# Row additions of one expert two in flight, pair lists fetched by ScalarE, last stage in place: a decoder layer with a sparse expert stage

## What is computed

```python
logits = flat @ router_w.T
scores = jax.nn.softmax(logits, axis=-1)
_, topk_idx = jax.lax.top_k(logits + router_bias, TOPK)
topk_scores = jnp.take_along_axis(scores, topk_idx, axis=-1)
topk_scores = topk_scores / topk_scores.sum(-1, keepdims=True)
combine = jnp.einsum('nk,nke->ne', topk_scores, jax.nn.one_hot(topk_idx, N_EXPERTS, dtype=scores.dtype))
out = jnp.zeros_like(flat)
for e in range(N_EXPERTS):
    h = jax.nn.silu(flat @ Wu[e]) * (flat @ Wg[e])
    out = out + combine[:, e:e + 1] * (h @ Wd[e])
out = out + jax.nn.silu(flat @ Su[0]) * (flat @ Sg[0]) @ Sd[0]
x = _layernorm(x + out.reshape(B, T, D), axis=-1)
```

## Time and profile before

| | |
|---|---|
| median of three runs (lowest, highest) | 2169.67 us (2161.83, 2170.12) |
| the profiled execution's own time, its span | 2160.96 us, 2159.3 us |
| stage 1, stage 2, stage 3 in the profile | to 1596, to 2106.8, to 2159.3 us |
| PE busy over the span | 1878.9 us (87%) |
| POOL busy; its idle time before L1407 | 767.0 us (36%); 152.8 us |
| ACT busy, DVE busy | 651.8 us (30%), 1194.9 us (55%) |
| additions, gathers, pair lists on POOL | 80 each; 1615, 983, 952 ns of POOL each |
| bytes moved in stage 3 | 16.79 MB |

### The profile page before, as it was taken

How to read it: one execution, slowest core, us unless ns; L and a number is a source line. 1 busy time by engine, 2 the same in 40 slices (tenths; PEclk the granted TensorE clock), 3 DMA queues, 4 the chain that set the end, 5 groups by cost and what they waited for, 6 DMA issues and landing times. The chain is left out here.

```text
span 2159.3 us, 35007 instructions
## 1 busy us (share of the span) xinstructions
PE 1878.9 (87%) x11010; PEld 1190.8 (55%) x11011; DVE 1194.9 (55%) x2460; ACT 651.8 (30%) x1357; POOL 767.0 (36%) x831
## 2 busy tenths in 40 slices
PE   3878999999999999999999999998759999999950
PEld 2456575766657566575766657576534544445420
DVE  2567776677667666766667676676422222222214
ACT  0152332424234242333424233241302212212214
POOL 3124233242323324233232323222235655655520
PEclk8889999999999999999999999998889999999985
DMA  7244243433423444142433424332035576565538
GB/s 235 55 111 105 53 103 78 105 99 66 115 61 94 103 91 115 40 115 71 94 99 84 115 59 96 83 82 60 21 156 110 125 197 170 90 149 114 94 52 311
DMA packets 142245, 225.35 MB, mean 104 GB/s; under 512 B 23360, under 2 KB 98112, under 8 KB 139456
## 3 DMA queue, kind: packets, MB, share of 16 engines
q1 hardware_dynamic: 101616, 132.94, 24.3%
q0 software_dynamic: 40528, 91.41, 18.2%
HBM read 94.70 MB, written 47.25 MB: 66 GB/s over the span
## 5 line engine op out<-in xcount | busy, mean ns | idle before, releaser
L1502 PE MATMUL ps<-ug_w,rowsT 128*128 x640 | 293.0, 601 | 6.8 <-SPq L1377 4.5
L1502 PEld LDWEIGHTS ps<-ug_w,rowsT 128*128 128x128 f32 x640 | 122.9, 193 | 163.0 <-issue 163.0
L950 DVE RECIPROCAL arden<-ps 128x256 f32<-128x256 f32 x64 | 112.5, 1758 | 143.8 <-PE ps L1274 140.3
L1017 PE MATMUL ps<-wqkv_sb,xT_sb 128*128 128x256 f32 (+1 forms) x512 | 173.7, 493 | 15.5 <-ACT maskr_sb L520 15.5
L1407 POOL DMA_INDIRECT sum_rows<-y_sb,pairs x80 | 129.2, 1615 | 152.8 <-DMA sum_rows<-y_sb,pairs 120.6
L470 POOL DMA_INDIRECT routed_ids<-pair_w,pos_w x64 | 64.0, 1000 | 328.2 <-DVE pair_w L741 291.0
L1458 DVE SCALAR_TENSOR_TENSOR silu<-tanh,ps 128x256 f32<-128x256 f32 x80 | 33.7, 421 | 256.3 <-ACT tanh L1425 256.3
L922 DVE SCALAR_TENSOR_TENSOR weighted<-ps,decay 128x384 f32<-128x384 f32 x256 | 140.4, 554 | 63.0 <-PE ps L1143 48.0
L905 DVE TENSOR_REDUCE smax<-ps 128x2 f32<-128x512 f32 x256 | 164.0, 682 | 17.0 <-PE ps L1200 17.0
L637 ACT ACTIVATE probs<-ps 128x1024 f32<-128x1024 f32 x128 | 130.9, 1025 | 116.2 <-PE ps L1251 116.1
L616 ACT ACTIVATE decay<-ps,g_col 128x256 f32<-128x256 f32 x256 | 121.6, 475 | 134.8 <-PE ps L1126 89.4
(11 more groups left out here) (239 smaller groups left out, 3913.4 us busy)
## 6 DMA issues: line engine op xcount, KB each, us to landing
q_stack<-qkT_hi SPq DMA_DIRECT2D x128, 128.0 KB, 3.8
mk_stack<-ctxT_hi SPq DMA_DIRECT2D x128, 128.0 KB, 4.9
mq_stack<-qkT_hi SPq DMA_DIRECT2D x128, 128.0 KB, 2.5
ug_w<-in_expert_ug SPq DMA_DIRECT2D x16, 1024.0 KB, 6.1
xT_sb<-in_xT SPq DMA_DIRECT2D x16, 512.0 KB, 3.4
x_sb<-in_x POOLq DMA_DIRECT2D x16, 512.0 KB, 4.0
ctxT_sb<-in_ctxT POOLq DMA_DIRECT2D x16, 512.0 KB, 3.7
q_stack<-qkT_lo SPq DMA_DIRECT2D x64, 128.0 KB, 4.4
```

Source lines behind the costliest of these rows:

```text
L950: nc.vector.reciprocal(arden[:, :], ps[:, 6 + c % 2, cols]).then_inc(arden_done.sem, 1)
L1017: ins = nc.tensor.matmul(ps[:, 2 * t + lo // 512, 0:hi - lo], xT_sb[:, c, P * t:P * t + P], wqkv_sb[:, c, lo:hi], start=c == 0, stop=c == ...
L1502: ins = nc.tensor.matmul(ps[:, 2 + k % 2, :], rowsT[:, k % 2, c, :], ug_w[:, bass.ds(slot, 1), c, :].rearrange("p o n -> p (o n)"), start= ...
```

## The change

**Additions.** Two semaphores `ey_added0` and `ey_added1` take turns, by the parity of the tile. Addition m waits until addition m - 2 has landed, and for m - 1 up to a number that stands in a new table `turns`: 16 times the additions of the other parity up to m - 3 where tile m belongs to the same expert as m - 1, and one more where the expert changes or where tile m is past the last used one. So with the 74 used tiles 59 additions need not wait for the one right before, and 21 must (or are the first): the 15 where an expert begins, and the six unused ones at the end, 74 to 79, which all go to the same spare rows. POOL reads the table's value from SBUF before each addition. LAG becomes 5.

**Pair lists.** Those of tiles 4 to 79 (and of four more that nobody uses) are fetched by ACT with a plain transfer at an address read from a new table `row0`; ACT issues it at the beginning of turns 0 to 3, and behind the copy of `rowsT` from turn 4 on. A gather waits for the new semaphores `later_in`.

**Tables.** DVE makes a third diagonal; PE's product (L1113) is 384 columns wide instead of 256; ten small operations for `row0` and `turns` are added behind the one that writes `idx`. `scored` and `ranks` move into the spare end of `hid`.

**Last stage.** `normalise` writes into `total` itself, and its wait for an earlier store is gone.

```diff
@@ -105,7 +105,8 @@
         def sem(name):
             return keep.enter_context(nc.semaphore(name))
 
-        tables = Tables(id_sb=sb("id_sb", [P, P]), idx=sb("idx", [P, MT], I32), pairs=sb("pairs", [P, MT, 2], I32),
+        tables = Tables(id_sb=sb("id_sb", [P, P]), idx=sb("idx", [P, MT], I32), pairs=sb("pairs", [P, MT + W, 2], I32),
+                        row0=sb("row0", [1, MT + W], I32), turns=sb("turns", [1, MT], I32),
                         weights=sb("weights", [1, MT], I32), slot=sb("slot", [1, MT], I32), ends=sb("ends", [1, E], I32),
                         pairs_in=[sem(f"pairs_in{q}") for q in range(W)], base_out=Signal(sem("base_out"), 16))
...
@@ -202,6 +203,8 @@
         hid_flat = hid[:, :, :, :].rearrange("p t h d -> p (t h d)")
         rope_a = hid_flat[:, 0:QKH * ROT].rearrange("p (h d) -> p h d", d=ROT)
         rope_b = hid_flat[:, QKH * ROT:2 * QKH * ROT].rearrange("p (h i two) -> p h i two", i=ROT // 2, two=2)
+        scored, ranks = (hid_flat[:, ST * H * HD - q * TOPK * ST * E:ST * H * HD - (q - 1) * TOPK * ST * E]
+                         .rearrange("p (k t e) -> p k t e", k=TOPK, e=E) for q in (1, 2))
         sq_flat = sq[:, :, :, :].rearrange("p t h d -> p (t h d)")
...
-                    for k in range(2):
+                    for k in range(3):
                         v.tensor_scalar(diag[:, k, :], id_sb[:, :], table[:, k:k + 1], None, ALU.mult).then_inc(diag_done.sem, 1)
 
...
                     dve.wait_ge(across_ready.sem, 1)
-                    v.tensor_copy(across, ps[:, 1, 0:2 * P].rearrange("p (k m) -> p k m", m=P)).then_inc(diag_done.sem, 1)
-                    dve.wait_ge(diag_done.sem, 3)
+                    v.tensor_copy(across, ps[:, 1, 0:3 * P].rearrange("p (k m) -> p k m", m=P)).then_inc(diag_done.sem, 1)
+                    dve.wait_ge(diag_done.sem, 4)
                     v.tensor_scalar(tables.idx[:, :], across[:, 0, 0:MT], row_p[:, :], None, ALU.add).then_inc(tables_done.sem, 1)
+                    v.tensor_copy(tables.row0[:, :], across[0:1, 0, 0:MT + W])
                     v.tensor_scalar(tables.weights[:, :], across[0:1, 1, 0:MT], 1.0, None, ALU.add)
+                    v.tensor_scalar(tables.ends[:, :], tiles_end[0:1, :], 1.0, None, ALU.add)
+
+                    v.tensor_tensor(change[:, 1:MT], across[0:1, 2, 1:MT], across[0:1, 2, 0:MT - 1], ALU.subtract)
+                    v.tensor_scalar(unused, across[0:1, 2, 0:MT], float(E - 1), None, ALU.subtract)
+                    v.tensor_scalar(half_i, iota_sb[0:1, 0:MT], 1.0, None, ALU.subtract)
                     v.tensor_copy(owner_i, across[0:1, 1, 0:MT]).then_inc(diag_done.sem, 1)
-                    v.tensor_scalar(tables.ends[:, :], tiles_end[0:1, :], 1.0, None, ALU.add)
-                    dve.wait_ge(diag_done.sem, 4)
+                    dve.wait_ge(diag_done.sem, 5)
                     v.tensor_scalar(tables.slot[:, :], owner_i, W - 1, None, ALU.bitwise_and)
+                    v.tensor_scalar(half_i, half_i, 1, None, ALU.arith_shift_right)
+                    v.tensor_tensor(change[:, 1:MT], change[:, 1:MT], unused[:, 1:MT], ALU.max).then_inc(diag_done.sem, 1)
+                    dve.wait_ge(diag_done.sem, 6)
+                    v.tensor_scalar(change[:, 1:MT], change[:, 1:MT], 0.0, 1.0, ALU.max, ALU.min).then_inc(diag_done.sem, 1)
+                    v.tensor_copy(unused, half_i).then_inc(diag_done.sem, 1)
+                    dve.wait_ge(diag_done.sem, 8)
+                    v.tensor_tensor(change[:, 1:MT], change[:, 1:MT], unused[:, 1:MT], ALU.add).then_inc(diag_done.sem, 1)
+                    dve.wait_ge(diag_done.sem, 9)
+                    v.tensor_scalar(tables.turns[:, 1:MT], change[:, 1:MT], 16.0, None, ALU.mult)
 
                 def hidden(c):
 
...
@@ -1109,8 +1126,8 @@
                     for c in range(1, SC):
                         ug(c)
                     if b is None and y is None:
-                        pe.wait_ge(diag_done.sem, 2)
-                        nc.tensor.matmul(ps[:, 1, 0:2 * P], ones_k[:, 0:1].to_broadcast([P, P]), sq_flat[:, 0:2 * P],
+                        pe.wait_ge(diag_done.sem, 3)
+                        nc.tensor.matmul(ps[:, 1, 0:3 * P], ones_k[:, 0:1].to_broadcast([P, P]), sq_flat[:, 0:3 * P],
                                          start=True, stop=True).then_inc(across_ready.sem, 1)
...
 
-    LAG = 7
+    LAG = 5
     with ExitStack() as ctx:
         def sb(name, shape, dt=F32):
...
+        later_in = [sem(f"later_in{s}") for s in range(W)]
 
         block = ctx.enter_context(nc.Block())
...
@@ -1392,29 +1410,37 @@
         def _(pool):
 
             def gather(m):
-                pool.wait_ge(tables.pairs_in[m % W], 16 * (m // W + 1))
-                if m >= W:
+                if m < W:
+                    pool.wait_ge(tables.pairs_in[m], 16)
+                else:
+                    pool.wait_ge(later_in[m % W], 16 * (m // W))
                     pool.wait_ge(rowsT_ready, m - W + 1)
                 pool.indirect_dma_start(out=rows[:, m % W, :], out_offset=None, in_=x2_dram,
                                         in_offset=bass.IndirectOffsetOnAxis(ap=tables.pairs[:, m, 0:1], axis=0)).then_inc(rows_in[m % W], 16)
 
             def add_up(m):
-                pool.wait_ge(y_done, m + 2)
-                if m >= 1:
-                    pool.wait_ge(y_added, 16 * m)
+
+                if m in (1, 2):
+                    pool.wait_ge(y_added[(m - 1) % 2], 16)
+                elif m > 2:
+                    turn = pool.value_load(tables.turns[0:1, m:m + 1], min_val=16, max_val=16 * MT)
+                    pool.wait_ge(y_added[m % 2], 16 * (m // 2))
+                    pool.wait_ge(y_added[(m - 1) % 2], turn)
                 else:
                     pool.wait_ge(tables.base_out.sem, 16 * B)
+                pool.wait_ge(y_done, m + 2)
                 pool.indirect_dma_start(out=sum_dram, out_offset=bass.IndirectOffsetOnAxis(ap=tables.pairs[:, m, 0:1], axis=0),
-                                        in_=y_sb[:, m % W, :], in_offset=None, compute_op=ALU.add).then_inc(y_added, 16)
+                                        in_=y_sb[:, m % W, :], in_offset=None, compute_op=ALU.add).then_inc(y_added[m % 2], 16)
 
             for m in range(MT + LAG):
                 if m < MT:
                     gather(m)
-                if m + W < MT:
-                    fetch_pairs(pool, ids_dram, tables, m + W)
                 if m >= LAG:
                     add_up(m - LAG)
-            pool.wait_ge(y_added, 16 * MT)
+            for s in range(2):
+                pool.wait_ge(y_added[s], 16 * (MT // 2))
+            for s in range(W):
+                pool.wait_ge(later_in[s], 16 * (MT // W))
 
         @block.scalar
         def _(act):
@@ -1437,13 +1463,24 @@
                     act.wait_ge(ug_ready, m - 1)
                 nc.scalar.copy(rowsT[:, k % 2, :, :], ps[:, k % 2, :].rearrange("p (c r) -> p c r", r=P)).then_inc(rowsT_done, 1)
 
+            def fetch(m, k):
+
+                of_m = slice(m, m + 1) if isinstance(m, int) else bass.ds(m, 1)
+                row = act.value_load(tables.row0[0:1, of_m], min_val=0, max_val=E * N)
+                pairs = tables.pairs[:, of_m, :].rearrange("p o two -> p (o two)")
+                act.dma_start(pairs, ids_dram[bass.ds(row, P), :]).then_inc(later_in[k % W], 16)
+
             def step(n, k):
+                if isinstance(n, int) and n < W:
+                    fetch(n + W, k + W)
                 if has(n, 1):
                     tanh(n - 1, k - 1)
                 if has(n, 2):
                     copy_hidT(n - 2, k - 2)
                 if has(n, 0):
                     copy_rowsT(n, k)
+                if not isinstance(n, int) or W <= n < MT:
+                    fetch(n + W, k + W)
 
             steps(act, step, 2)
...
-                    dve.wait_ge(y_added, 16 * (m - W + 1))
+                    rounds = (m - k) * 8 if not isinstance(m, int) else 0
+                    dve.wait_ge(y_added[k % 2], rounds + 16 * ((k - W) // 2 + 1))
                 of_row = share[:, m, :] if isinstance(m, int) else share[:, bass.ds(m, 1), :].rearrange("p o u -> p (o u)")
                 v.tensor_scalar(y_sb[:, k % W, :], ps[:, 4 + k % 2, :], of_row, None, ALU.mult).then_inc(y_done, 1)
...
 def finish(nc, sum_dram, out):
 
-    G, O = 4, 2
+    G = 4
...
-        result = sb("cresult", [P, O, G, D])
         total_in = [sem(f"ctotal_in{g}") for g in range(NT // G)]
-        out_sem = [sem(f"cout{s}") for s in range(O)]
+        out_sem = sem("cout")
         own_step, aggregated = sem("cown_step"), sem("caggr")
         var_done, dev_done, shift_done, normed = sem("cvar_s"), sem("cdev_s"), sem("cshift_s"), sem("cnormed")
...
-                sp.dma_start(out_v[:, G * g:G * g + G, :], result[:, g % O, :, :]).then_inc(out_sem[g % O], 16)
-            for s in range(O):
-                sp.wait_ge(out_sem[s], 16 * (NT // G // O))
```

(27 more changed lines are left out.)

## The result

Six runs of the changed kernel took 2137.69 to 2145.01 us, median 2141.43; six of the kernel before, 2161.83 to 2170.12, median 2164.56. The ratio is 0.9886 with a 95% interval from 0.9871 to 0.9902: 24.7 us faster (21 to 28). I had forecast 12.3 us and a range that began at 2144. The direction was right, the size was not.

A forecast was written before the change was run, and what follows sets the result against it. Stage 2 was taken as bound by PE at 5.80 us a tile, hiding the 5.61 us addition chain, stage 3 by transfers, then a buffer wait. From 2165.6, -5.3 - 7.3 + 0.3 = -12.3 gave 2153.3 us; range 2144 to 2167.

The forecast's parts named there:

- The additions, -5.3 us: End of stage 2: two additions in flight remove a one-tile lag, so the last goes 5.3 us earlier; bounds 0 to 12.6.
- the additions set the upper level: Stage 2: slower transfers make the chain outlast PE's turn, costing 8 us over 80 tiles; 2148.7 in all runs; chance 0.15.
- The gathers behind additions at LAG 5, 0 us: Stage 2: gathers queued behind additions still arrive within 7.7 us of room; cost nothing, 0 to 4 us for the range.
- POOL's shorter turn, 0 us: Stage 2: POOL loses 76 pair lists and gains a table read per addition, all in spare time; worth nothing.
- The fetch on ACT, 0 us: Stage 2: each pair-list fetch takes ACT about 1.0 us, at most 4.1, hidden in its free 4.57 us.
- The tables, +0.3 us: Table building ahead of `idx`: wider product copy adds 0.3 us, from 0 to 1; ten operations hide in DVE's wait.
- Stage 3, -7.3 us: Last stage: without the buffer wait transfers set the end, so the last store lands 7.3 us earlier; bounds 5 to 7.9.
- the rival of 375 for the stores: Stage 3: stores run at 375 GB/s, not 408, so the gain is 10.5 us, the time 2155.1; chance 0.05.
- the rival on gathers: Stage 2: gathers late at 12 weight loads halt PE, 3.8 us each, 45.6 us in all, giving 2203; chance 0.04.
- the rival on ACT's fetch: Stage 2: the fetch outlasts ACT's 4.57 us, each tanh 0.3 us late, 23 us over 76 tiles; chance 0.03.

The follow-up runs named there:

- e6: The changed kernel with 256 spare rows, neighbouring tiles using different halves, unused tiles two in flight; ratio to before 0.9889, in a second run 0.9894.
- e10: The kernel before without the weight loads of experts 4 to 15, whose tiles multiply by older weights; ratio 0.9909, 19.9 us faster.
- r_before: The kernel before, unchanged, run again against itself; ratio 0.9987.
- e1_last_stage: The kernel before with only the new last stage in place; ratio 0.9954, 10.0 us faster.
- e2_ranks: The kernel before with only `scored` and `ranks` moved into the spare end of `hid`; ratio 1.0.
- e4_fetch: The changed kernel with every addition serial, LAG 7 and the old last stage; ACT's pair lists and the tables remain; ratio to before 1.0009.
- e3_adds: The changed kernel with pair lists fetched by POOL again and the old last stage; ratio to before 0.9943, 12.4 us faster.
- e5_serial: The changed kernel with every addition waiting for the one before, LAG 5; median 2173.19 us, ratio to before 0.9984.
- r_after: The changed kernel, unchanged, measured again; median 2162.09 us, ratio to before 0.9934, 14.4 us faster.
- r_after2: The changed kernel, unchanged, a third time, on another chip; ratio to before 0.99, 21.8 us faster.
- e7: The changed kernel with LAG 7 instead of 5; ratio to before 0.9933.

## Why the prediction was wrong

The pieces of the profiles, without those of e6 and e10, in us:

| | to PE's last up product | to the last addition | to stage 3 | stage 3 |
|---|---|---|---|---|
| before, serial | 477.5 | 23.1 | 9.9 | 52.4 |
| r_before, serial | 477.4 | 29.7 | 9.9 | 52.1 |
| e1_last_stage, serial | 479.1 | 32.4 | 9.7 | 45.0 |
| e2_ranks, serial | 476.1 | 28.7 | 9.7 | 52.7 |
| e4_fetch, serial, ACT fetches | 477.1 | 28.8 | 8.2 | 52.4 |
| e3_adds, two in flight | 476.9 | 18.5 | 9.7 | 52.3 |
| e5_serial, serial, ACT fetches, LAG 5 | 482.7 | 20.5 | 7.8 | 45.6 |
| after, r_after, r_after2, e7 | 477.1 to 478.1 | 18.5 to 18.7 | 8.1 to 8.2 | 45.5 to 46.0 |

**The additions, -5.3 us: the step that failed.** The prediction read that "the chain is one tile late when PE ends" and took "the value from the rows of this very place". The mechanism was right, the size was that of one execution. At LAG 7 serial additions end 23.1, 28.7, 28.8, 29.7 and 32.4 us after PE's last up product begins, a mean of 28.5; with two in flight it is 18.5 to 18.7 in five profiles. The term is 10.0 us and not 5.3, and the profile that I had lay at the favourable end. (In e5_serial a part of the lag went into PE's own way, so it is not in this mean.) The lag is no tile that is lost at the end but what the weight loads have left over, 6.1 us at tile 74 in one profile and 12.3 in the other. Each value is of one execution, and whether the chip or the execution decides it is open. The prediction named what makes the lag differ: 0.19 us of room a tile, and weight loads that add 3 to 4 us each. Twelve loads against so little room cannot end at a fixed lag; that should have widened the term to the depth of the four buffers. I gave 0 to 12.6 as its bounds, but carried them into the range only in part.

**The rival "the additions set the upper level"**, at 0.15, came nearest in size, with its 21 us, and was right that the additions cost more than 5.3. Its mechanism was not what the traces show, so the nearness is in part luck: it had all 80 tiles slower, and PE's way to its last up product is 476 to 477.5 us in four of the five serial profiles at LAG 7 (479 in one); the loss is at the end. Its sum was loose too: 3% of 5.61 is 0.17 us, less than the room of 0.19, and 8 us over 80 tiles needs a chain 5% longer. Whether the lag explains before's two levels was not tested run by run.

**The gathers behind additions at LAG 5, 0 us:** right. In the changed kernel there is no wait of PE for rows, and LAG 7 gives the same time, although an addition waited up to 7.7 us at a load. The prediction's own worst case, 6 us and 4.2 more, was above its room of 7.7 and did not come; with serial additions PE does wait for rows here and there (e5_serial).

**POOL's shorter turn, 0 us:** right for the steady part, wrong at the end: 1.7 us in the drain, which stood in no row of mine and in no term.

**The fetch on ACT, 0 us:** right. It takes 1.2 us and not 1.0, with 3.4 us left: its table read has a median of 0.81 us where PE's had 0.30. The Trainium skill's floor of about 600 ns ("DMA: Bandwidth & Descriptors", Latency and other measured facts) is nearer to ACT's median, and the 0.28 to 0.30 us that ACT, PE and POOL all reach lie under it.

**The tables, +0.3 us:** not visible, and no run shows the term. The copy takes 0.55 and not 0.42 us, the ten operations 2.2, and DVE still waits for PE behind them. On stage 1 alone the difference is 1.5 us, within its scatter.

**Stage 3, -7.3 us:** right, -6.4 in the two profiles and -7.4 in e1. The end is the transfers', at 409 GB/s in the window of the last issue; with loads and stores together they ran at 384 to 389 GB/s, with stores alone at 406 to 410, so the rival of 375 for the stores fell.

**Sum.** 10.0 + 1.7 + 6.8 (52.4 to a mean of 45.6) - 0.3 = 18.2 us, of which the 0.3 is the prediction's own. Three comparisons gave 24.7 (21 to 28), 14.4 (8.5 to 20.4) and 21.8 (15.0 to 28.6), a mean of 20.3. The first lies 6.5 us above the pieces, as much as the two profiles' first stages differ; since stage 1 alone shows no gain, I put it to scatter, and that was not shown for those runs themselves. So the pieces account for 6 us more than the 12.3 of the forecast; the cause of the last 6.5 us of the first measurement stays open. The starting point was also high: 2165.6 from four times, where six gave 2164.6.

**Slips in the sums.** The additions' steps as written give 5.2 and not 5.3 us. The 2203 of the rival on gathers stands on the median of before; on 2165.6 it is 2199. In the rival on ACT's fetch 23 us on 2148.7 are 2171.5 and not 2164. None of them moves the forecast by more than 0.1 us.

## What to carry to other kernels

A chain that hides behind another engine by 3% has no fixed cost: it keeps most of every delay that anything adds, up to the depth of its buffers, and shows it at the end of the stage (here 21 undisturbed tiles gave back under 3 us). One profile shows one draw of that; size the term by the buffers (here four results) and by the count of disturbances, or take several profiles of the kernel before. Additions that can't meet on a row need no order among each other, and what must stay serial at the end of a stage costs its full latency each.

## What the runs showed that I had not expected

The drain of GpSimd at the end of stage 2 was longer where it had issued more indirect transfers there: 2.83 and 2.84 us with 160, 4.59 and 4.64 with 236, by my estimate 23 ns for each of the 76 pair lists more. A read of one number from SBUF into a register took 0.29 us in the median on GpSimd, 0.30 on TensorE and 0.81 on ScalarE. And the first stage, with or without the new tables, ended between 1590 and 1614 us over the profiles, so that differences under 10 us between single profiles of such a kernel must be read piece by piece.
